# A transformer block with per-sample modulation: the prologue's loads and small computations put in the order of their first use

## The reference, cut to what matters

```python
mod = (silu(c) @ wmod).reshape(B, 6, 1, -1)          # c: 2 x 256, wmod: 256 x 1536
sa, ca, ga, sb, cb, gb = (mod[:, k] for k in range(6))
ga = (2 * (ga >= 0) - 1) * maximum(abs(ga), 0.25)    # gates; gb alike
h = layernorm(x) * (1 + ca) + sa
x = x + ga * attention(h)    # q, k, v = h @ W + b; per head the 307 queries with the largest
                             # max - mean of scores attend over all keys; the others give zero
h = layernorm(x) * (1 + cb) + sb
x = x + gb * experts(h)      # soft dispatch to 8 experts x 128 slots; the slot vectors are
                             # sn = slot / max(norm(slot), 1e-12) * 16 * slot_gamma
```

## Time and profile before

| | |
|---|---|
| median of 3 runs | 1737.82 us (1734.71 to 1747.33) |
| the profiled execution | 1734.49 us, its span 1732.4 us |
| busy share | PE 87%, DVE 68%, ACT 59%, GpSimd (POOL) 17% |
| mean granted TensorE clock | 0.958 of full |
| prologue until the first unit | 0 to 48.0 us |
| units and value tiles of sample 0 | 48.0 to 116.3 us |
| first product of `maxima(0)` | 123.4 us |

### The profile page before, as it was taken

How to read it: one execution, slowest core, us unless ns; L and a number is a source line. 1 busy time by engine, 2 the same in 40 slices (tenths; PEclk the granted TensorE clock), 3 DMA queues, 4 the chain that set the end, 5 groups by cost and what they waited for, 6 DMA issues and landing times.

```text
span 1732.4 us, 27920 instructions
## 1 busy us (share of the span) xinstructions
PE 1513.4 (87%) x8112; PEld 826.5 (48%) x8114; DVE 1177.2 (68%) x2943; ACT 1018.2 (59%) x1364; POOL 302.0 (17%) x363
## 2 busy tenths in 40 slices
PE   2779999998859999999998869979799899989989
PEld 1442222223435542222223635534588786468878
DVE  3659999999767849999999869846333343632211
ACT  2338888887736668888886447643333372333243
POOL 1370000001633444000000214431111000011100
PEclk7889999999989999999998989989899999989999
DMA  9441112112321121111112112120044202014410
GB/s 246 164 128 35 38 38 51 39 37 73 128 92 54 52 67 38 37 46 45 37 47 75 56 38 54 53 66 0 34 150 138 85 30 70 0 53 149 138 40 30
DMA packets 91780, 119.11 MB, mean 69 GB/s; under 512 B 21346, under 2 KB 77378, under 8 KB 91204
## 3 DMA queue, kind: packets, MB, share of 16 engines
q1 hardware_dynamic: 88644, 117.73, 22.8%
q0 software_dynamic: 3072, 0.66, 0.4%
HBM read 93.54 MB, written 24.78 MB: 68 GB/s over the span
## 4 chain that ended last, share of the span: by engine, by line
PE 46%; DVE 31%; issue 13%; ACT 4%; DMA 3%; SPq 1%; POOL 1%; DVEq 0%; PEld 0%; ACTq 0%; POOLq 0%; PEldq 0%
DVE work_area L1060 23%; PE psum L1745 7%; PE psum L1806 6%; PE psum L1619 4%; PE psum L1642 4%; PE psum L1715 4%; PE psum L1631 4%; PE psum L1753 3%; PE psum L1769 3%; PE psum L1474 2%; DVE big_area L1060 2%; PE psum L1798 2%; PE psum L1562 1%; ACT big_area L794 1%; DVE work_area L1134 1%
## 5 line engine op out<-in xcount | busy, mean ns | idle before, releaser
L1060 DVE CUSTOM_DVE_ANT_0 work_area<-psum,work_area 128x1024 f32<-128x1024 f32 x512 | 589.5, 1220 | 17.2 <-PE psum L1521 13.3
L728 ACT ACTIVATE work_area<-psum 128x1024 f32<-128x1024 f32 x512 | 510.3, 1026 | 86.3 <-DVE big_area L1060 33.3
L1521 PE MATMUL psum<-work_area 96*128 96x512 bf16 x1024 | 311.1, 386 | 47.9 <-DVE big_area L1060 7.6
L1511 PE MATMUL psum<-work_area 96*128 96x512 bf16 x1024 | 308.2, 383 | 13.6 <-DMA work_area<-q_parts 7.2
L746 ACT ACTIVATE work_area<-psum 128x614 f32<-128x614 f32 x256 | 163.9, 681 | 78.4 <-PE psum L1631 78.3
L1521 PEld LDWEIGHTS psum<-work_area 96*128 96x128 bf16 x1024 | 64.1, 98 | 267.0 <-DVE big_area L1060 249.9
L1511 PEld LDWEIGHTS psum<-work_area 96*128 96x128 bf16 x1024 | 89.3, 98 | 160.9 <-ACT work_area L728 58.6
L603 POOL DMA_INDIRECT heads_out<-work_area x96 | 98.6, 1027 | 146.5 <-DVE work_area L1217 125.5
L1188 DVE TENSOR_SCALAR big_area<-iota,rank 128x308 bf16<-128x308 f16 x512 | 122.4, 312 | 0.0
L1745 PE MATMUL psum<-xn,work_area 128*128 128x257 f32 x512 | 117.4, 388 | 4.7 <-ACT work_area L812 4.7
L1715 PE MATMUL psum<-slots_T,work_area 128*128 128x512 f32 x256 | 116.6, 600 | 2.9 <-ACT work_area L790 2.9
(11 more groups left out here) (229 smaller groups left out, 1910.2 us busy)
## 6 DMA issues: line engine op xcount, KB each, us to landing
work_area<-in_L_ffn_w_dram SPq DMA_DIRECT2D x32, 1024.0 KB, 5.3
work_area<-q_parts SPq DMA_DIRECT2D x192, 64.0 KB
k_parts<-work_area SPq DMA_DIRECT2D x24, 384.0 KB, 3.2
work_area<-k_parts SPq DMA_DIRECT2D x32, 192.8 KB
q_parts<-work_area SPq DMA_DIRECT2D x16, 384.0 KB, 2.6
big_area<-q_parts SPq DMA_DIRECT2D x16, 384.0 KB, 7.0
work_area<-k_parts SPq DMA_DIRECT2D x32, 192.0 KB
work_area<-k_parts SPq DMA_DIRECT2D x32, 128.5 KB
```

The lines of the kernel that those rows point to most:

```text
L728: s.activation(SC[:, t % 4], PS[:, 2 * (n % 2):2 * (n % 2) + 2].rearrange("p a n -> p (a n)"), ACT.Relu).then_inc(relu_done, 1)
L1060: v.tensor_tensor_reduce(SC[:, t % 4], PS[:, 4 + 2 * (t % 2):6 + 2 * (t % 2)].rearrange("p a n -> p (a n)"), SC[:, t % 4], 1.0, -3.0e38, A ...
L1511: last = mm(PS[:, 2 * (n % 2) + k], QS1[par][0:TERMS, t * P:(t + 1) * P], KS[par][0:TERMS, k * 512:(k + 1) * 512], start=True, stop=True)
L1521: last = mm(PS[:, 4 + 2 * (t % 2) + k], QS1[par][0:TERMS, t * P:(t + 1) * P], KS[par][0:TERMS, K1 + k * 512:K1 + (k + 1) * 512], start=Tru ...
```

## The change

What is moved, split or replaced:

- SP's loads: c, the shift and scale columns of wmod (0 to 511), token group 0, Wq and Wk with their bias columns, groups 1 and 2, the other columns of wmod, group 3, slots, Wv. The later parameters, sample 1, the zero rows and `b1s` go between or behind the units' parts.
- `modC` is no longer read back from DRAM: eight products with wmod as the stationary operand and silu(c) as the moving one (two columns) put it in PSUM as columns.
- The other four modulation rows, the slot squares, roots, rows and transposes are computed between the units: on TensorE behind u = 3, 10 and 13, on ScalarE behind u = 3, 6 and 11 to 14, on VectorE behind u = 3, 5 and 8; the four gates are behind u = 11, 12, 15 and 16.
- Moments and deviations of the tokens are made group by group; group 0's deviations have their own square root. `setup_done` is gone; each use has its own wait.
- The three key loads of a head are six of 16 partitions each, for every head.

The diff, without declarations:

```diff
@@ block.sync
-            sp.dma_start(wmods, wmod...).then_inc(cond_in, 16)
-            sp.dma_start(X[:, 0], x_v[0]).then_inc(x_in[0], 16)
-            (slots, Wq, Wk, Wv, Wo, bias columns, five rows, b1s -> params_in;
-             mod_rows out and back as modC and modR; X[:, 1]; zeros)
+            sp.dma_start(wmods[:, :, 0:2 * D], wmod_v[:, :, 0:2 * D]).then_inc(mods_in, 16)
+            tokens(0)
+            weights_in(Wqs[:], Wq, qk_in)
+            weights_in(Wks[:], Wk, qk_in)
+            for dst, src in ((bqc, bq), (bkc, bk)):
+                sp.dma_start(dst[:], ...).then_inc(qk_in, 16)
+            tokens(1)
+            tokens(2)
+            sp.dma_start(wmods[:, :, 2 * D:], wmod_v[:, :, 2 * D:]).then_inc(more_mods_in, 16)
+            tokens(3)
+            sp.dma_start(slotN, ...).then_inc(slots_in, 16)
+            sp.dma_start(slotG, rowv(slot_gamma)).then_inc(slots_in, 16)
+            weights_in(Wvs[:], Wv, v_in)
+            sp.dma_start(bvB[:], rowv(bv)).then_inc(v_in, 16)
...
                 for n in (3, 2, 1):
-                    sp.dma_start(KS[par][at:at + n * DH, 0:K1 + HALF], k_parts[b][0:n, bass.ds(h0, DH), 0:K1 + HALF]).then_inc(kq_in[par], 16)
-                    at += n * DH
+                    for r in range(n):
+                        sp.dma_start(KS[par][at:at + DH, 0:K1 + HALF], k_parts[b][r, bass.ds(h0, DH), 0:K1 + HALF]).then_inc(kq_in[par], 16)
+                        at += DH
...
             for u in range(NU):
                 parts_to_dram(0, u)
+                if u == 3:
+                    mod_rows_out()
+                if u == 5:
+                    mod_rows_in()
+                if u == 7:
+                    late_params()
+                if u in (8, 9, 10, 11):
+                    at = (u - 8) * G
+                    sp.dma_start(X[:, 1, at:at + G], x_v[1][:, at:at + G]).then_inc(x1_in, 16)
             first_heads(0)
+            zero_rows()
+            expert_bias()
             other_heads(0)
@@ block.scalar
+            first_deviations()
+            act.wait_ge(modc_ready, 1)
+            other_deviations()
             take_tokens(0, 0)
             for u in range(NU):
                 first_part(0, u)
+                if u == 3:
+                    slot_squares()
+                if u == 6:
+                    slot_roots()
+                if 11 <= u < 15:
+                    take_slots(u - 11)
@@ block.vector
+            dve.wait_ge(x_in[0], 16)
+            first_moments(group_tiles(0), early_var)
+            mod_columns()
+            dve.wait_ge(early_sqrt, 1)
+            refine(G, rstd[:, 0:G], 1.0)
             normalised(0)
+            for g in range(1, NG):
+                dve.wait_ge(x_in[g], 16)
+                first_moments(group_tiles(g), var_ready if g == NG - 1 else None)
+            (constants)
+            dve.wait_ge(sqrt_done, 1)
+            refine(NT, rstd[:, G:], 1.0, G)
             for u in range(NU):
-                if opens(u):
-                    if UNITS[u][0] < NG - 1:
-                        normalised(UNITS[u][0] + 1)
-                    gate(UNITS[u][0] // 2, 3 * (UNITS[u][0] % 2))
+                if opens(u) and UNITS[u][0] < NG - 1:
+                    normalised(UNITS[u][0] + 1)
                 split_units(0, range(u, u + 1))
+                if u == 3:
+                    row_mods()
+                if u == 5:
+                    slot_spread()
+                if u == 8:
+                    slot_rows()
+                    row_scales()
+                if u in (11, 12, 15, 16):
+                    gate(u // 15, 3 * (u % 4 == 0))
@@ block.tensor
-            for k in range(3):
-                for cc in range(DC):
-                    last = mm(PS[0:B, k], silT[:, cc], wmods[:, cc, k * 512:(k + 1) * 512], ...)
+            pe.wait_ge(mods_in, 16)
+            for k in range(2):
+                for co in range(DC):
+                    for cc in range(DC):
+                        last = mm(PS[:, 5, (k * DC + co) * B:(k * DC + co + 1) * B], wmods[:, cc, k * D + co * P:k * D + (co + 1) * P], silT[:, cc], ...)
...
+            def turn_slots(quarters):
+                pe.wait_ge(sn_ready, 1)
+                pe.wait_ge(modc_ready, 2)
+                pe.wait_ge(mod_done, 1)
+                for k in quarters:
+                    (four transposes of slot rows into bank 5 + k % 3)
...
                 last.then_inc(qk_ready, 1)
+                if b == 0 and u == 3:
+                    row_mods()          # four products of 512 columns, then VectorE copies them
+                if b == 0 and u in (10, 13):
+                    turn_slots(range(3) if u == 10 else (3,))
                 if g < NG - 1 and opens(u):
                     turn_tokens(b, g + 1)
...
+            pe.wait_ge(v_in, 32)
+            pe.wait_ge(snT_done, 4)
             for t in range(NT):
                 value_tile(0, t)
```

More of the change, by code:

```diff
@@ L186, in adaln_block @@
         LS = Area(big).take([NT, M])
-        sqS = Area(big).take([E, D])
-        work = sb("work_area", [P, 12160])
-        a = Area(work)
+        a = Area(big, values_end)
         wmods = a.take([DC, 6 * D])
@@ L194, in adaln_block @@
         silT = a.take([DC, B])
-        modrow = a.take([6 * D])
+        modrow = a.take([4 * D])
         slotN = a.take([E, D])
@@ L199, in adaln_block @@
         selh = a.take([P])
+        sqS = a.take([E, D])
+        work = sb("work_area", [P, 12160])
         a = Area(work)
@@ L335, in _, with tokens, weights_in @@
         def _(sp):
+            wmod_v = wmod.rearrange("(c p) n -> p c n", p=P)
+            def tokens(g):
+                at = group_tiles(g)[0]
+                sp.dma_start(X[:, 0, at:at + G], x_v[0][:, at:at + G]).then_inc(x_in[g], 16)
+            def weights_in(dst, src, landed):
+                sp.dma_start(dst, src.rearrange("(c p) n -> p c n", p=P)).then_inc(landed, 16)
             for k in range(B):
                 sp.dma_start(cT[:, :, k], c[k].rearrange("(c p) -> p c", p=P), allow_slow_non_contiguous=True).then_inc(cond_in, 16)
-            sp.dma_start(wmods, wmod.rearrange("(c p) n -> p c n", p=P)).then_inc(cond_in, 16)
@@ L357, in _ @@
[L357 to L361, removed]
-            sp.wait_ge(zeros_ready, 1)
-            for b in range(B):
-                hz = heads_out[b].rearrange("(p j) d -> p (j d)", p=P)
-                for k in range(2):
-                    sp.dma_start(hz[:, k * 2048:(k + 1) * 2048], zeros).then_inc(zero_out, 16)
+            sp.dma_start(wmods[:, :, 0:2 * D], wmod_v[:, :, 0:2 * D]).then_inc(mods_in, 16)
@@ new lines, in late_params, with expert_bias, zero_rows @@
+            def late_params():
+                weights_in(Wos[:], Wo, late_in)
+                for dst, src in ((boB[:], bo), (gamB[:], gamma)):
+                    sp.dma_start(dst, rowv(src)).then_inc(late_in, 16)
+            def expert_bias():
+                sp.dma_start(b1s[:], b1.rearrange("e (j p) -> p e j", p=P), allow_slow_non_contiguous=True).then_inc(late_in, 16)
+            def zero_rows():
+                sp.wait_ge(zeros_ready, 1)
+                for b in range(B):
+                    hz = heads_out[b].rearrange("(p j) d -> p (j d)", p=P)
+                    for k in range(2):
+                        sp.dma_start(hz[:, k * 2048:(k + 1) * 2048], zeros).then_inc(zero_out, 16)
```

184 lines of the change are left out of this document (106 added, 78 removed).

## The result

The changed kernel takes 1729.6 us (median of 6 runs, 1723.54 to 1732.09) against 1741.91 us for the kernel before in the same session (6 runs, 1734.71 to 1747.33): ratio 0.993, 95% interval 0.9907 to 0.9953. It is faster, by 12.3 us where 25 were forecast, and outside the range. On two other chips, beside its own runs of before, it gave 0.9926 twice. The profiled execution after took 1723.54 us (span 1721.4), 10.95 less than that of before; it is the fastest of its six runs.

What follows compares the result with a forecast made beforehand. The late start of the search for maxima was taken as the bound: 24.3 us sooner plus 1.0 from the clock gives 25.3, a profiled 1709.2 us and a median forecast of 1712, range 1701 to 1724.

Steps and rivals of the forecast that it cites:

- the search's start: First product of the search for maxima: at 99.1 us instead of 123.4, 24.3 us sooner.
- the gates: In the units, u = 11 to 16: four gates on VectorE, mostly absorbed, add 2.7 us (0.5 to 5).
- the wait for the loads' issue: From the units' end to the first head's load issue: 8.6 us, against 7.6 before.
- Until the first unit: Before the units: first unit at 20.2 us instead of 48.0, set by the wait for group 3's moments.
- Rival 3: Group 3 does not hold the start, small terms vanish: first unit 3 us sooner, gain 34, 1704 us; chance 0.11.
- The units: The 20 units: 54.3 us plus 8 (4 to 12) for work moved into them, ending at 82.5.
- slot work: In the units: slot roots, rows and scales behind u = 8 add 4.1 us (3 to 5).
- From the last unit to the search: Units' end to first search product: issue begins 8.6 us later, twelve issues take 5.5, landing 2.5; start at 99.1.
- rival 2: At the search's key loads: more pieces land no faster, landing stays 8.4 us, gain 18.4, 1719 us; chance 0.10.
- The clock: At the search's start: TensorE stands less, so its clock may not fall; 1.0 us gained (0 to 2.7).
- Rival 1: In the units: VectorE becomes the bound and absorbs gain, leaving 16 to 18 us, 1720 us; chance 0.17.
- Rival 4: Behind the first heads: moved writes (zero rows, b1) delay the next heads' loads; slower, say 1745 us; chance 0.03.

Runs made afterwards that it cites:

- e1: The changed kernel with the search's key loads joined again, three a head; 1750.37 us, 0.9936 of the kernel before.
- e2: The kernel before with only the search's key loads split in six; 1756.84 us, 0.9979 of the kernel before.
- e4: The changed kernel with the attention's key loads split in six as well; 1719.33 us, 0.9879 of the kernel before.
- n5: The kernel of e4 run again, on the same chip as n4; 1719.12 us, 0.9884 of the kernel before.
- n4: The changed kernel, unchanged, run again on the same chip as n3; 1727.33 us, 0.9926 of the kernel before.
- e10: e9 with ScalarE taking token group 0 ahead of the other groups' root; 1738.29 us, 0.9884 of the kernel before.
- n2: The changed kernel, unchanged, run again on another chip; 1749.73 us, 0.9926 of the kernel before.
- e8: The changed kernel with the four gates moved to the start of attention 0 and the attention's key loads split in six; 1733.1 us, 0.9857 of the kernel before.
- e9: e8 with slot roots, slot rows and row scales behind the units, slot transposes between the value tiles; 1736.9 us, 0.9884 of the kernel before.
- e6: The changed kernel with the four gates behind the last unit and the attention's key loads split in six; 1713.9 us, 0.9855 of the kernel before.
- n6: The kernel of e8 run again, on the same chip as n4; 1716.51 us, 0.9862 of the kernel before.
- e3: The changed kernel with the four gates behind the last unit, attention keys still joined; 1722.13 us, 0.9897 of the kernel before.
- n3: The kernel before, unchanged, run again on the same chip as n4; 1737.92 us (one run).

## Why the prediction was wrong

Right were the direction, why the start came late and several single terms. The time lost lies in two places of the program, up to the search and in attention 0, and the outcome, a gain under 17 us, had been given 0.04. Of the 24.3 us forecast for the search's start 4.0, 7.9 and 7.4 are missing in the three pairs of the table; attention 0 takes another 2.2, 4.8 and 4.2.

*The step that failed behind the search's start* is the first one of the prediction: "Behind 123 us nothing of the program differs but the number of key loads, so what counts is how much earlier the search for maxima begins." The number of key loads counts behind it too. I priced their issue for head 2 of search 0 (rightly hidden: 124.98, needed later) and put at nothing, without a reason, what the same loads do at the next place where they occur, beside the joined loads of attention 0's last head. There the step to head 15 takes 11.25 to 12.74 us in after for 9.08 to 10.06 in before, and e1, e2, e4 and n5 show it from four sides. n5 wins 8.2 us over n4 and not 4, since other steps of attention 0 fall to 7.95 as well (8.17 to 8.55 in n4); in the two traces attention 0 differs by 6.9 us.

*The terms that were mis-sized up to the search* are the gates (priced at 2.7) and the wait for the loads' issue (8.6, measured 12.3 to 12.5), as follows.

*Until the first unit:* 20.85 for 20.2. Group 3 and not group 0 sets it, as the ScalarE rows and e10 show. Rival 3, that the start could be 3 us sooner and keep it, is refuted by e10 as a gain: the wait only moves to group 1.

*The units:* 62.4 us for 62.3 in the first trace, 8.1 more than before, but 65.7 and 64.8 in n2 and n4, 11.7 more each. That the first trace met the sum is luck. Wait for the slot rows and for group 3: 3.50 and 1.01 for "about 3 and 2". Taking the slot work out (e8 to e9) gives 5.4, priced at some 5. The gates were priced at 2.7: out of the units they give 6.8 from e4 to e6 and 6.1 from n4 to n6, but 2.0 from e4 to e3. Of this 4.1 are the wait for the mean key; the rest, up or down, goes by where the half clock falls. I had taken the 0.43 us of an instruction that ran without GpSimd beside it and moved all four gates to where GpSimd is at work. What is left without slot work and gates, 51.9 us in e9, is 2.4 less than before's 54.3, and that hid it; why it is less is open.

*From the last unit to the search:* load issue comes 12.5 us behind the units' end, not 8.6 (12.3 and 12.5 in n2 and n4). VectorE's last casts of the units end at 88.4, 5.2 us behind the units' end and some 3 later than before, of which I had priced 1. And the last store lands 4.8 us behind its issue, where before's last took 2.9. With the gates out of the units the issue comes 8.1 behind (e8) and that store lands 2.9 behind its issue; why it is slower with them is open. Twelve issues take 5.4 for 5.5, landing 2.0 behind the last one needed for 2.5: right, and rival 2 is refuted (e1, e2). The old landing was 8.7 by the rows, not the 8.4 of the prediction; nothing hangs on it. The Trainium skill ("DMA: Bandwidth & Descriptors", "Why a DMA increments its semaphore by 16 and not by 1") gives 3 and 2 engines to the two larger joined key loads and 16 to a split one; the share of 0.15, 2.4 engines, agrees, and 0.52, 8.3 engines, is more than 3 could give. The rule of the Trainium skill on the same page ("Bandwidth"), to batch to 1 MiB, would have spoken against splitting; here 64 KB pieces landed sooner. The clock gave 0.9 us in the first pair, for 1.0, and 0.2 in the second, and took 0.4 in the third.

In the pair n3, n4: 16.5 at the fourth reduction, less 4.2 in attention 0, with small changes after, makes 12.1 at the end; the medians say 13.6 in that session and 12.3 in the first. Rival 1 (gain 16 to 18 from VectorE) is about what happened up to the search; it had 0.17. Rival 4 did not occur: zero rows and b1 were issued by 111.4. The chance of a change within 1%, given as 0.13, comes to some 0.16 by the prediction's own words (0.04, and nearly half of 0.27).

*Open:* the 7.6 and 4.9 us that go between attention 0's end and the 33rd exponential of attention 1 in two of the three pairs. Stretches of half clock lie there whose place differs between executions of one kernel; whether the changed start shifts their odds wasn't settled by three traces of each.

## To carry to other kernels

When a helper is called in several stages, price the change at each call, beside what is queued there; the price at the first call is not that of the next. A load that is spread over more engines can hold up a load that was issued just ahead of it on few engines: here the gain was kept only when both were split. And take an instruction's duration from a stretch in which the same neighbours work as at its new place.

## Seen of the hardware

- VectorE beside GpSimd: with two inputs in SBUF `SCALAR_TENSOR_TENSOR` 128x256 took 1.28 to 1.37 us for 0.43, and `TENSOR_SCALAR`, with one, 1.24 for 0.29. With one input in PSUM `SCALAR_TENSOR_TENSOR` 128x512 kept its 0.75, wholly beside GpSimd's two instructions of 29.87 to 32.54:

```profile
31.34 0.74 DVE L1077 SCALAR_TENSOR_TENSOR work_area<-psum,bk_col,work_area 128x512 f32<-128x512 f32 x1
```

  The Trainium skill ("SBUF — State Buffer", "Who interferes with whom") says that VectorE and GpSimd share a pair of ports, and that a VectorE instruction with two SBUF inputs contends with GpSimd's reads, one with at most one SBUF input outside the fast modes doesn't. The rows of `SCALAR_TENSOR_TENSOR` agree; those of `TENSOR_SCALAR` do only if it runs in a fast mode, which no row names.
- On two of the four chips of the experiments ScalarE stands once in nearly every head of attention 0, in before as in the changed kernels, at a granted clock of 1.00, and a step is 9.1 us instead of 7.95. ScalarE in e8, where it happens, and in e4, where it doesn't:

```profile
569.65 1.89 ACT L797 ACTIVATE work_area<-psum 128x614 f32<-128x614 f32 x3 [2.44 <-PE psum L1750]
```

```profile
568.06 1.25 ACT L797 ACTIVATE work_area<-psum 128x614 f32<-128x614 f32 x2 [0.85 <-PE psum L1747]
```

  In e8 the two attentions take 24.8 us longer than in n6, the same kernel on a chip without it, and the whole 18.4; the cause wasn't found. Splitting the attention's keys was expected to remove it and doesn't (e8). The ratio of after to before did not depend on it (0.9926 on either kind of chip).
- A short stretch of half clock costs 1.57 us in a head (steps 8.70 and 9.07 us for 7.13 and 7.50). TensorE in after, attention 1, the same products at half clock, then at full, and the window of the first:

```profile
1020.70 1.25 PE L1757 MATMUL psum<-work_area 128*32 128x307 f32 x8
...
1024.27 0.72 PE L1757 MATMUL psum<-work_area 128*32 128x307 f32 x8
```

```profile
1020.40:1023.80 3.40, 3.40 (x18) 1.66 (x17) 2.25 (x9) 1.09 (x2) 1.51 (x2) 0.50 0.15 44
```
